# A graph convolution and mixture-of-experts kernel: fewer dense groups, a later turn of a group's sum, experts' rows stored during the norm

## The reference

```python
def gcn_conv(x, src, dst, w, W, b, n):
    xw = x @ W
    deg = jax.ops.segment_sum(w, dst, num_segments=n)
    dinv = jnp.where(deg > 0, jax.lax.rsqrt(deg), 0.0)
    norm = dinv[src] * w * dinv[dst]
    out = jax.ops.segment_sum(xw[src] * norm[:, None], dst, num_segments=n)
    return out + b
...
    out = relu(gcn_conv(x, src, dst, w, W1, b1, n))
    out = gcn_conv(out, src, dst, w, W2, b2, n)
    out = (out - mean) * rsqrt(var + BN_EPS) * gamma + beta
    return relu(out + identity)
...
    top2_vals, top2_idx = jax.lax.top_k(softmax(xf @ gate_w + gate_b), 2)
    # per expert: h = gelu(xf @ w1 + b1); y = h @ w2 + b2; acc + we * y
...
    x = x + gnn(layernorm(x))
    x = x + ffn(layernorm(x))
```

## Time and profile before

| | us |
|---|---|
| median of 3 runs | 2776.79 |
| lowest, highest | 2775.86, 2789.46 |
| the profiled execution | 2760.07 |
| its span | 2758.3 |
| TensorE busy | 2008.3 (73%) |
| GpSimd busy | 1699.3 (62%) |
| VectorE busy | 899.0 (33%) |
| ScalarE busy | 424.7 (15%) |

### The profile page before, as it was taken

The page is one execution under the profiler, slowest core; times in us unless marked ns, Lnnn a source line. Parts: engine busy times, 40 slices in busy tenths (PEclk is TensorE's granted clock), DMA queues, the critical chain, the costliest instruction groups (busy, mean ns, idle before and its releaser), DMA issues.

```text
span 2758.3 us, 29927 instructions
## 1 busy us (share of the span) xinstructions
PE 2008.3 (73%) x8514; PEld 1397.0 (51%) x8515; DVE 899.0 (33%) x2676; ACT 424.7 (15%) x1140; POOL 1699.3 (62%) x1679
## 2 busy tenths in 40 slices
PE   0353249887778886665688888888885473999998
PEld 0251014444445444554445555554554362899997
DVE  7970001111122113342113323232323776333332
ACT  1610000000000000111000000000000465344443
POOL 2887732566656666665765666755665544566665
PEclk6555559988889987878889999998998555999999
DMA  9993013454445443334444545544545313688885
GB/s 321 336 312 101 27 40 124 135 165 152 147 138 168 147 151 103 119 117 119 142 148 143 175 154 170 158 145 141 170 154 186 101 58 129 179 209 207 214 210 137
DMA packets 263529, 431.17 MB, mean 156 GB/s; under 512 B 38800, under 2 KB 147023, under 8 KB 263279
## 3 DMA queue, kind: packets, MB, share of 16 engines
q1 hardware_dynamic: 180591, 253.79, 27.8%
q0 software_dynamic: 81088, 173.80, 23.8%
q10 hardware_dynamic: 1728, 2.13, 0.2%
HBM read 339.36 MB, written 91.16 MB: 156 GB/s over the span
## 4 chain that ended last, share of the span: by engine, by line
another core or an unknown queue 34%; PE 28%; issue 17%; DVE 13%; DMA 3%; ACT 1%; SPq 1%; POOL 1%; DVEq 1%; POOLq 0%; ACTq 0%
PE psum L1508 8%; PE psum L1679 6%; PE psum L1687 6%; PE psum L1554 4%; DVE arena L1122 3%; DMA arena<-pair_weights 1%; DMA out_dram<-ACC 1%; PE psum L1467 1%; SPq L453 1%; PE psum L1670 1%; DVE edge_cols L1214 1%; DVE stats L1220 1%; PE psum L1526 1%; DVE ACC L926 1%
## 5 line engine op out<-in xcount | busy, mean ns | idle before, releaser
L575 POOL DMA_INDIRECT arena<-conv_rows,edge_cols x1120 | 1065.3, 951 | 694.3 <-issue 338.7
L1508 PE MATMUL psum<-arena,X 128*128 128x512 f32 x1568 | 805.7, 636 | 220.5 <-issue 141.4
L1554 PE MATMUL psum<-arena 128*128 128x256 f32 x2240 | 595.3, 399 | 78.2 <-issue 64.8
L1554 PEld LDWEIGHTS psum<-arena 128*128 128x128 f32 x2240 | 447.1, 203 | 271.1 <-issue 218.1
L1508 PEld LDWEIGHTS psum<-arena,X 128*128 128x128 f32 x1568 | 314.6, 202 | 512.8 <-issue 434.4
L1146 DVE TENSOR_TENSOR ACC<-ACC,psum 128x256 f32 x80 | 33.8, 422 | 1037.9 <-remote 441.5
L560 POOL DMA_INDIRECT pair_weights<-scale_b,mean_b x224 | 252.3, 1126 | 116.7 <-issue 67.9
L1122 DVE TENSOR_SCALAR arena<-iota,edge_cols 128x128 f32<-128x128 f32 x1120 | 298.1, 359 | 6.1 <-issue 5.9
L650 POOL DMA_INDIRECT out_dram<-ACC x105 | 166.3, 1583 | 108.9 <-DMA out_dram<-ACC 78.3
L729 ACT ACTIVATE arena<-psum 128x256 f32<-128x256 f32 x80 | 30.4, 380 | 1311.7 <-remote 727.5
L1679 PE MATMUL psum<-ACC,arena 128*128 128x128 f32 x1680 | 208.3, 277 | 0.2 <-DVE ACC L1356 0.2
(11 more groups left out here) (287 smaller groups left out, 1532.4 us busy)
## 6 DMA issues: line engine op xcount, KB each, us to landing
arena<-pair_weights SPq DMA_DIRECT2D x329, 256.0 KB
arena<-in_L_ffn_W_dram SPq DMA_DIRECT2D x113, 512.0 KB, 7.9
pair_weights<-zeros SPq DMA_DIRECT2D x4, 12544.0 KB, 44.2
arena<-conv_rows,edge_cols POOLq DMA_INDIRECT x1120
arena<-pair_weights SPq DMA_DIRECT2D x9, 1792.0 KB
conv_rows<-X SPq DMA_DIRECT2D x14, 896.0 KB
X<-in_x_dram SPq DMA_DIRECT2D x12, 896.0 KB
rows_for_experts<-ACC SPq DMA_DIRECT2D x7, 910.0 KB, 4.2
```

The costliest lines, as they stand in the source:

```text
L575: pool.indirect_dma_start(G[:, n * D:(n + 1) * D], None, y_tab[layer], bass.IndirectOffsetOnAxis(srcT[:, t:t + 1], 0)).then_inc(gathered[n ...
L1508: ins = m.matmul(bank(6 + c, BW), X[:, t * D + c * P:t * D + (c + 1) * P], table, start=(t == 0), stop=(t == NT - 1))
L1554: ins = m.matmul(bank(2 * (k % 2), D), S[:, n * P:(n + 1) * P], G[:, n * D:(n + 1) * D], start=(j == 0), stop=(j == GT - 1))
```

## The change

Four of the dense groups become gathered ones: DG = 12, NB = 3, UNITS = 147, GG = 44. There are three fills and 168 scatters in the front, 42 units run there, and per layer 49 units fewer and four gathered groups more are left. PER_GROUP is 3.5 units per group in layer 0 and 4 in layer 1. In layer 0 the units then end in group 29.

SUM_TURN is 7. DVE's loop is written anew to fit: in step k it first waits for sum k-1, builds the matrices of group k+1, adds a block where one is due, adds group k-1 and then does the finishes; it added group k last before.

In the tail ACT computes the experts' rows no second time. SP stores the 256 words of a row from `acc` right after `n_ready` of a chunk, in two DMAs of 128 x 7 x 128 words, and ACT's `copy_turned`, which overwrites them, waits for the store. The last chunk's transposed rows go to a buffer of their own, `last_turned`. The choices are stored alone, in one DMA of 128 x 49 x 4 words. POOL's copies go. In the 14 steps POOL does c % 3 == 1 only, and ACT takes c % 3 == 2, in seven small activations.

```diff
-DG = 16
+DG = 12
...
-        XN = late(2 * CH * DX)
+        last_turned = late(CH * D)
...
-        BEFORE = (63, 0)
+        BEFORE = (42, 0)
...
-        PER_GROUP = ((5, 1), (16, 3))
+        PER_GROUP = ((7, 2), (4, 1))
...
-        SUM_TURN = 2
+        SUM_TURN = 7
...
                         sp.dma_start(out[(NT - 1) * P:N, :], X[0:TAIL, t0:t0 + D]).then_inc(total_set, 16)
-
-                for c in range(NCH):
-                    sp.wait_ge(xn_ready, CH * (c + 1))
-                    sp.wait_ge(choice_in, c + 1)
-                    r0 = (c % 2) * CH * DX
-                    sp.dma_start(rows_of(rows_x, c), tile3(XN[:, r0:r0 + CH * DX])).then_inc(xn_stored[c % 2], 16)
+                    sp.wait_ge(n_ready, CH * (c + 1))
+                    for k in range(KC):
+                        sp.dma_start(rows_of(rows_x, c)[:, :, k * P:(k + 1) * P],
+                                     tile3(acc[:, k, c * CH * P:(c + 1) * CH * P])).then_inc(xn_stored[c % 2], 16)
+                sp.wait_ge(choice_set, 1)
+                sp.dma_start(rows_x[0:NP, D:DX].rearrange("(t p) d -> p t d", p=P), tile3(choice, NT)).then_inc(choice_in, 16)
 
...
-                pool.wait_ge(choice_set, 1)
-                for c in range(NCH):
-                    if c >= 2:
-                        pool.wait_ge(xn_stored[c % 2], 16 * (c // 2))
-                    g.tensor_copy(tile3(XN[:, (c % 2) * CH * DX:(c % 2 + 1) * CH * DX])[:, :, D:DX],
-                                  choice[:, 4 * CH * c:4 * CH * (c + 1)].rearrange("p (t k) -> p t k", k=4)
-                                  ).then_inc(choice_in, 1)
-
...
-                for c in range(2 * NCH):
-                    if c % HOTS == 0:
-                        continue
+                for c in range(1, 2 * NCH, HOTS):
...
-                    pool.wait_ge(xn_stored[n], 16 * SLOT_CH[n])
+                    pool.wait_ge(xn_stored[n], 32 * SLOT_CH[n])
+                pool.wait_ge(choice_in, 16)
...
                 def copy_turned(c):
+                    act.wait_ge(xn_stored[c % 2], 32 * (c // 2 + 1))
                     for j in range(CH):
...
 
-                def expert_rows(c):
-                    if c >= 2:
-                        act.wait_ge(xn_stored[c % 2], 16 * (c // 2))
-                    for j in range(CH):
-                        n, t = (c % 2) * CH + j, CH * c + j
-                        a.activation(XN[:, n * DX:n * DX + D], X[:, t * D:(t + 1) * D], ACT.Identity,
-                                     bias=nmr[:, t:t + 1], scale=rstd[:, t:t + 1]).then_inc(xn_ready, 1)
-
                 def places(c):
...
                     act.wait_ge(hot_at, c + 1)
-                    a.activation(node[:, :, 0], at.rearrange("p n t -> p t n"), ACT.Copy,
-                                 scale=place[:, 0:1]).then_inc(hot_place, 1)
-
-                for c in range(NCH - 2):
-                    expert_rows(c)
+                    ins = a.activation(node[:, :, 0], at.rearrange("p n t -> p t n"), ACT.Copy, scale=place[:, 0:1])
+                    if c % HOTS == 2:
+                        for t in range(CH):
+                            ins = a.activation(node[:, t, 1], at[:, :, t], ACT.Copy, scale=float(c % NCH * CH + t + 1))
+                    ins.then_inc(hot_place, 1)
+
                 for c in range(2 * NCH):
                     places(c)
-                    if c in (2, 5):
-                        expert_rows(NCH - 2 + c // 3)
 
...
                             if k + 1 < GG:
+                                if k:
+                                    dve.wait_ge(summed, GG * layer + k)
                                 build(k + 1)
...
                                 blocks += 1
+                            if k:
+                                add_group(k - 1)
                             if layer == 1 and k and 0 in FINISH[1][1][k - 1]:
...
                                 finish(layer, i)
-                            add_group(k)
+                        add_group(GG - 1)
                         dve.wait_ge(added, GG * (layer + 1))
...
-                    v.tensor_copy(acc[:, :, q * P:(q + 1) * P], turned(j).rearrange("p (c n) -> p c n", c=KC)
-                                  ).then_inc(n_copied, 1)
+                    v.tensor_copy(last_turned[:, j * D:(j + 1) * D], turned(j)).then_inc(n_copied, 1)
...
+                for n in range(2):
+                    dve.wait_ge(xn_stored[n], 32 * SLOT_CH[n])
...
+                    at = (q - (NCH - 1) * CH) * D
...
-                        m.matmul(bank(2, T8)[:, q * NX:(q + 1) * NX], acc[:, k, q * P:(q + 1) * P],
+                        rows = acc[:, k, q * P:(q + 1) * P] if at < 0 else last_turned[:, at + k * P:at + (k + 1) * P]
+                        m.matmul(bank(2, T8)[:, q * NX:(q + 1) * NX], rows,
...
-                    if c % HOTS:
-                        pe.wait_ge(hot_tile, c - c // HOTS)
+                    if c % HOTS == 1:
+                        pe.wait_ge(hot_tile, c // HOTS + 1)
```

More of the change, by code:

```diff
@@ L277, in gnn_ffn @@
         member_set, rank_done = sem("member_set"), sem("rank_done")
-        xn_ready, choice_set, choice_in = sem("xn_ready"), sem("choice_set"), sem("choice_in")
+        choice_set, choice_in = sem("choice_set"), sem("choice_in")
         xn_stored = [sem(f"xn_stored{n}") for n in range(2)]
```

## The result

The changed kernel takes 2824.31 us (median of 4 runs, 2821.56 to 2836.38), the kernel before 2776.32 in the same measurement. The ratio is 1.0188, with a 95% interval from 1.0146 to 1.0229: **slower by 1.9%**, where 1.3% faster was forecast. The time lies in the range, next to the price of the rival whose slow stretches stay (2825). That nearness is luck in part: the rival's sum gave a span of 2806.8 us, and the profiled execution of after took 2836.38 us with a span of 2834.6. So the two traces differ by 76 us where the medians differ by 48.

The account below looks back on a forecast made before the run. TensorE's slow stretch while POOL scatters, then POOL's gather loop waiting for late sum signals, bound it; 357.4 + 53.0 + 559.7 + 241.8 + 74.4 + 807.7 + 638.1 - 10 = 2722.1 us span, median 2741, range 2675 to 2830.

Parts of the forecast that it names:

- slow stretches stay: Rival: TensorE still hits its record limit and groups come late, means staying 20.58 and 20.86; median 2825 us; chance 0.22.
- The front: Stretch before the first gather: 56 fewer scatters, slow rate (2.8 us a TensorE record) ending at 326.4, first gather 103.4 us earlier.
- What becomes of p0 and p1: Mean times per gathered group with units in layer 0 (p0) and per layer 1 group (p1): 19.3 and 19.7 us.
- the limit of 75: In the gathered groups: 75 records after a POOL pause, TensorE falls to the slow rate of 2.8 us a record.
- It loses nothing: DVE's new wait for sum k-1 before building group k+1 costs nothing; the old order reached the build 1.2 us after that signal.
- light groups: Layer 0's gathered groups without units: 12 instead of 11, at an unchanged 20.15 us each, 241.8 us.
- The rival that POOL never waits: Gathered groups: sum-to-signal is a fixed 8.4 us lag, sums come in time, 17.55 us a group; median 2602 us; chance 0.11.
- The tail: After the last groups: POOL's small copies go, expert table and product come 9.3 us earlier, stores mostly hidden; 10 us gained.
- The turn does nothing: Case: moving the sum's turn has no effect, only records per group count; median 2780 us, no chance of its own.
- The 20.35 at which it was to decide: Mean us per group from which the eight added groups have eaten what front and tail give.

## Why the prediction was wrong

**The front** was right in mechanism and near in size on its chip: 107.3 us for 103.4. The slow rate ended at 317.3, 11.6 us behind the last scatter's start, where I took 19.8 and 326.4. But with prompt signals gather 0 follows the last scatter at once: 306.65, the last scatter having begun at 305.4, and 378.05 in the version with 16 dense groups and the new tail. So there the front gives the 56 scatters, 70.4 us by count, and no more.

**What becomes of p0 and p1** is the step that failed: 19.3 and 19.7 us a group were forecast, 20.23 and 21.12 came. Its count of records was right: 44 a group in layer 0, as measured (1279 in 29), sums did pass under POOL's stream, and TensorE's stand at the turn went. From that I concluded triples, in which one group without a pause stands between two with a pause of 2.8 us. The trace shows pairs of 17.7 and 22.2 or so instead: the pause behind each group that passed is 5 us and more. As I read it, two groups of 44 records come close to the limit of 75, and a sum that is under way there is late by more than the 2.8 us of a regular pause; that is argued, no run showed it. I had weighed the second sum at 66 to 76 records against 75 and booked it as passing.

**"It loses nothing"** of DVE's new order was wrong: I followed the sum's signal to the turn and not the turn's own signal to the add. With the turn at tile 2 that signal mostly fell in just behind POOL's pause and passed; it was held in 12 of 80 groups, and in 25 of 88 with the turn at tile 7. The prediction named what is queued behind DVE's wait for the sum, and not what is queued behind its wait for the turn: finishes, and through them TensorE's linears. The light groups took 22.5 us each instead of 20.15, a term that I had booked as unchanged. Some of layer 1's 21.12 may be the same: 12 of the 25 held turns are there.

**The rival that POOL never waits** had the right eye on POOL and the wrong sign. I priced it from the late-signal trace, where it would have been a gain of 175 us for the change. But the kernel before has the same stream. Where signals are prompt POOL waits for sums in neither, and the difference is the count of indirect DMAs: 1344 before, 1400 after. That count was in the page and in the diff. It is the floor under both versions, and the change raises it by 70 us; what it lowers, TensorE's records, had slack in every later run that tried it (4 us and nothing for most of the units). On the first chip the count tells most of it as well. Of the 76 us by which the trace of after is longer, eight more groups at the old means cost 165, front and tail give back 123, and that leaves 42; the other 34 are what groups and layer change cost beyond the old means, 29 of them in the light groups.

**The tail** was right: 10 forecast, 11.7 in the first trace's last term, 9.6 alone. The reasons were right too: the stores hide in the norm loop (ACT waited 0.8 us for one), and POOL's table starts with its input.

**The turn does nothing** was listed as a case without a price of its own. On the later chips it comes near the truth: 0.1%, and that slower.

**The slow stretches stay** was the rival nearest to what the trace shows. Its sentence that one group comes late after two without a pause is seen in part, but its prices were the old ones, 20.58 and 20.86, and it left the light groups at 20.15. They came at 20.23, 21.12 and 22.5. That its median is within 1 us of the measured one is luck, as its span is 28 us short. The 20.35 at which it was to decide doesn't come out of the sum either: the old span of 2758.2 is reached at a mean of 20.05.

## What to carry to other kernels

Before costing waits, count the instructions of the engine that streams, before and after: a change that trades work of an engine with slack for work of the one that never stops loses the difference, here 63 us where the count says 70 - 10. When a signal is moved, follow each signal of the chain to its consumer, not only the first, and list what is queued behind each. A trace can be from a chip in a condition that the next run doesn't meet; a wait without a reason that the profile can name is a hint to price the case in which it isn't there, for both versions.

## What the runs showed of the hardware

In the first measurement TensorE's records came one in 2.8 us while POOL scattered (56 from 240.0 to 396.8 us), ACT's copy began 4.8 us behind a group's last product in the median (2.3 in the changed kernel), and DVE's add up to 24.5 us behind a turn. In all later runs, on chips 0, 1, 2 and 9, the copy began 0.04 us behind the product; in the version with the new groups alone the units ran beside the scatters in records of 0.592 us, and the kernel before took 2423 to 2428 instead of 2776 us, over 12% less. A group's 14 gathers without a pause took 17.5 us or a little more in both, and behind the last gather the times agree within 0.5 us. The cause is open.

In the kernel before with a pause in each group, a gather landed 2.1 us after POOL's last issue in the median of the groups without loads, and 3.9 us where 256 KB loads ran beside it; single groups took up to 5.8. A store of 6272 rows of 16 bytes landed in 9.0 to 11.1 us, one of 448 KB in runs of 512 bytes in 3.9 to 4.8.
